# Four-layer graph transformer on one core: when layer 1's head inverses, logit rows and layer 0's expert selectors are computed

## The reference

```python
scores = jnp.sqrt(jax.nn.softplus(flat @ gate_w))
_, indices = jax.lax.top_k(scores + gate_bias, K)          # K = 2 of E = 8
combine = combine.at[jnp.arange(N)[:, None], indices].add(weights)
gate_h = jnp.minimum(jnp.einsum('td,edi->eti', flat, w1), LIMIT)
up_h = jnp.clip(jnp.einsum('td,edi->eti', flat, w3), -LIMIT, LIMIT)
h = jax.nn.silu(gate_h) * up_h
routed = jnp.einsum('etd,te->td', jnp.einsum('eti,eid->etd', h, w2), combine)
```

```python
h = (x @ W).reshape(n, heads, out_c)
al_s = jnp.einsum('nhc,hc->nh', h, a_src)
al_d = jnp.einsum('nhc,hc->nh', h, a_dst)
e = jax.nn.leaky_relu(al_s[src] + al_d[dst], 0.2)
m = jax.ops.segment_max(e, dst, num_segments=n)
ex = jnp.exp(e - m[dst])
z = jax.ops.segment_sum(ex, dst, num_segments=n)
out = jax.ops.segment_sum(h[src] * (ex / (z[dst] + 1e-16))[:, :, None], dst, num_segments=n)
```

## Time and profile before

| | us |
|---|---|
| median of three runs (lowest, highest) | 3343.7 (3342.97, 3345.96) |
| the profiled execution, its own time | 3345.06 |
| its span in the trace | 3343.3 |
| TensorE busy | 3091.6 (92%) |
| VectorE busy | 1723.2 (52%) |
| GpSimd busy | 1425.0 (43%) |
| ScalarE busy | 757.8 (23%) |
| mean granted TensorE clock | 0.95 |

### The profile page before, as it was taken

One profiled execution on the slowest core, in us unless ns is written; L12 is line 12 of the kernel. 1 busy time (PEld: TensorE's weight loads), 2 busy tenths in 40 slices (PEclk: granted clock), 3 DMA queues, 4 the chain that ended last, 5 costly groups with the idle time before them and its releaser, 6 DMA issues.

```text
span 3343.3 us, 39028 instructions
## 1 busy us (share of the span) xinstructions
PE 3091.6 (92%) x14135; PEld 2440.7 (73%) x14145; DVE 1723.2 (52%) x2812; ACT 757.8 (23%) x1342; POOL 1425.0 (43%) x1007
## 2 busy tenths in 40 slices
PE   8999899999999976998987889899999998989978
PEld 3576577788888864776776578578888886778858
DVE  7734699465655355447775446533334436641131
ACT  1044211333333122103153121211111102221222
POOL 2022288344433451653520034356666664536500
PEclk9999999999999988999987789999999999999987
DMA  2011266112211231221210231122332222213313
GB/s 81 15 48 43 90 215 205 62 58 76 67 57 57 71 99 35 81 85 62 66 34 10 65 112 60 59 85 90 99 99 94 94 89 66 70 47 101 94 43 120
DMA packets 92134, 259.38 MB, mean 78 GB/s; under 512 B 10431, under 2 KB 11071, under 8 KB 91716
## 3 DMA queue, kind: packets, MB, share of 16 engines
q1 hardware_dynamic: 80352, 219.45, 20.8%
q10 hardware_dynamic: 11652, 38.19, 3.4%
HBM read 256.03 MB, written 1.57 MB: 77 GB/s over the span
## 4 chain that ended last, share of the span: by engine, by line
PE 83%; DVE 10%; issue 3%; ACT 2%; DMA 0%; ACTq 0%; DVEq 0%
PE ps L427 22%; PE ps L431 21%; PE ps L432 21%; PE ps L909 2%; DVE aux L1963 2%; PE ps L535 1%; PE ps L529 1%; PE ps L1229 1%; PE ps L1125 1%; PE ps L788 1%; PE ps L799 1%; PE ps L781 1%; PE ps L773 1%; DVE hot L2398 1%; DVE row L1773 1%
## 5 line engine op out<-in xcount | busy, mean ns | idle before, releaser
L365 POOL TENSOR_SCALAR w_hi<-raw 128x768 fp32r<-128x768 f32 x498 | 457.8, 919 | 1701.2 <-PE ps L427 1459.8
L368 POOL TENSOR_TENSOR w_lo<-raw,w_hi 128x768 fp32r<-128x768 f32 x498 | 975.3, 1958 | 41.5
L427 PE MATMUL ps<-H_hi,w_hi 128*128 128x512 f32 x804 | 319.0, 397 | 21.1 <-issue 11.6
L427 PE MATMUL ps<-A_hi,w_hi 128*128 128x512 f32 x780 | 308.7, 396 | 17.6 <-DVE sel_now L2235 17.6
L431 PE MATMUL ps<-H_lo,w_hi 128*128 128x512 f32 x804 | 315.8, 393 | 0.0
L432 PE MATMUL ps<-H_hi,w_lo 128*128 128x512 f32 x804 | 315.7, 393 | 0.0
L427 PE MATMUL ps<-B_hi,w_hi 128*128 128x512 f32 x720 | 291.8, 405 | 21.0 <-DVE B_lo L1757 14.9
L431 PE MATMUL ps<-A_lo,w_hi 128*128 128x512 f32 x780 | 305.5, 392 | 0.0
L432 PE MATMUL ps<-A_hi,w_lo 128*128 128x512 f32 x780 | 304.6, 391 | 0.0
L431 PE MATMUL ps<-B_lo,w_hi 128*128 128x512 f32 x720 | 283.3, 393 | 0.0
L432 PE MATMUL ps<-B_hi,w_lo 128*128 128x512 f32 x720 | 283.0, 393 | 0.0
(11 more groups left out here) (477 smaller groups left out, 5882.6 us busy)
## 6 DMA issues: line engine op xcount, KB each, us to landing
raw<-stream_dram SPq DMA_DIRECT2D x558, 384.0 KB, 3.0
w_ring<-w_dram ACTq DMA_DIRECT2D x45, 384.0 KB, 3.7
u_rows<-rows_dram ACTq DMA_DIRECT2D x8, 768.0 KB, 5.6
rows<-rows_dram ACTq DMA_DIRECT2D x7, 768.0 KB, 3.9
w_last<-w_dram ACTq DMA_DIRECT2D x9, 384.0 KB, 3.5
x<-x_dram ACTq DMA_DIRECT2D x1, 1536.0 KB, 9.1
out_dram<-x ACTq DMA_DIRECT2D x1, 1536.0 KB, 5.1
orf<-orf_dram ACTq DMA_DIRECT2D x6, 192.0 KB, 3.0
```

The costliest lines, as they stand in the source:

```text
L365: pool.tensor_scalar(w_hi[:, b // 3, b % 3], raw[:, b // 3, b % 3], 1.0, 1.0, ALU.mult, ALU.mult)\
L368: pool.tensor_tensor(w_lo[:, b // 3, b % 3], raw[:, b // 3, b % 3], w_hi[:, b // 3, b % 3], ALU.subtract)\
L427: mm = pe.matmul(o, wh, xh, start=first, stop=False, skip_group_check=True)
```

## The change

- `experts0`: the copy of `sel_now` stands in front of `gat_vectors` of blocks 0 to 3 on VectorE, in the first round.
- In the projection, the source rows come two at a time: heads 0, 1 and the columns behind chunk 3, heads 2, 3 behind chunk 5, heads 4, 5 in the middle of tile 4, heads 6, 7 behind tile 5. The first `gat_targets` (bank 1 instead of 7) stands in the middle of tile 5 and the rows of head 0 behind it; the columns use bank 5.
- The features then hold only the second `gat_targets` and the rows of heads 1 and 2. The rows of head 3 stand behind them as before. ScalarE makes head 0's exponentials ahead of the first feature copy, heads 1 and 2 behind the second and third.
- The inverse of head `h` stands behind the weights of head `h + 2` (before: `h + 3`, and none before head 3's), the scaling of head `h` behind the exponentials of head `h + 4` (before: `h + 3`).
- `e_slope` has four buffers. Which head takes which is `slope_of`. ScalarE waits for the last head that had the same one.
- The merge is one `scalar_tensor_tensor` (smaller than 1, then larger) in place of a `tensor_tensor` (larger).
- The blocks owed to GpSimd are given back by a 2 x 2 matmul ahead of `gat_head_rows`, not by the transposes of `gat_targets`.

```diff
+        e_slope = [lambda m: edge_w[1][:, m], lambda m: exp_1[m // 2][:, 4 + m % 2], lambda m: exp_02[0][:, m],
+                   lambda m: exp_02[1][:, m]]
+        slope_of = [0, 1, 0, 1, 2, 3, 0, 1]
...
+            def gat_head_rows(h):
...
+                    if owed[0]:
+                        pe.matmul(ps[0:2, b, 0:2], ones_b[:, :], ones_b[:, :], start=True, stop=True,
+                                  skip_group_check=True).then_inc(w_used, owed[0])
+                        owed[0] = 0
...
+                def beside_projection(f, half=False):
+                    if (f, half) == (4, True):
+                        gat_source(4)
+                        gat_source(5)
+                    if (f, half) == (5, True):
+                        gat_targets(0, 1)
+                    if (f, half) == (5, False):
+                        gat_source(6)
+                        gat_source(7)
+                        gat_head_rows(0)
...
             def gat_exps(h):
-                if h >= 2:
-                    act.wait_ge(exps_merged, NT * (h - 1))
+                before = [u for u in range(h) if slope_of[u] == slope_of[h]]
+                if before:
+                    act.wait_ge(exps_merged, NT * (before[-1] + 1))
...
+                gat_exps(0)
                 for u in range(2 * NT):
                     gat_feature(u)
-                    if u in (1, 3, 5):
-                        gat_exps(u // 2)
+                    if u in (1, 2):
+                        gat_exps(u)
                 mark(act_to_pe)
-                for h in range(3, GAT):
+                gat_exps(3)
+                for h in range(4, GAT):
                     gat_exps(h)
-                    gat_scaled(h - 3)
+                    gat_scaled(h - 4)
...
-                        dve.tensor_tensor(e, e, e_slope[h % 2](m), ALU.max).then_inc(exps_merged, 1)
+                        dve.scalar_tensor_tensor(out=e, in0=e, scalar=1.0, in1=e_slope[slope_of[h]](m), op0=ALU.min, op1=ALU.max)\
+                           .then_inc(exps_merged, 1)
...
-                gat_vectors(range(4))
-                experts("experts0", 2, 10.0, True, lambda i: gat_vectors(range(4, KC)) if i == 0 else None)
+                experts("experts0", 2, 10.0, True, lambda n: gat_vectors((range(4), range(4, KC))[n]) if n < 2 else None)
...
-                gat_weights(0)
-                gat_weights(1)
                 gat_targets(1, 4)
-                for h in range(2, GAT):
+                for h in range(GAT):
                     gat_weights(h)
-                    if h >= 3:
-                        gat_inverse(h - 3)
+                    if h >= 2:
+                        gat_inverse(h - 2)
```

More of the change, by code:

```diff
@@ L936, in gat_terms @@
             def gat_terms():
-                pe.wait_ge(logits_out, 1)
-                use(7)
+                use(5)
                 for m in range(NT):
-                    mm = pe.transpose(ps[:, 7, m * 16:m * 16 + 16], row[0:16, m * P:m * P + P], ident[0:16, 0:16])
-                done(mm, 7, "dve")
+                    mm = pe.transpose(ps[:, 5, m * 16:m * 16 + 16], row[0:16, m * P:m * P + P], ident[0:16, 0:16])
+                done(mm, 5, "dve")
             def gat_source(h):
                 b = 6 + h % 2
+                if h == 0:
+                    pe.wait_ge(logits_out, 1)
                 use(b)
@@ L1073, in _, with behind_chunk @@
                 gat_logits()
-                turn_t(H, "dve", since, last=False,
-                       behind_chunk=lambda k: gat_terms() if k == 3 else gat_source(k - 4) if k >= 4 else None,
-                       halfway=lambda f: gat_source(f - 1))
+                def beside_projection(f, half=False):
[8 more added lines that the diff above has]
+                        gat_head_rows(0)
+                def behind_chunk(k):
+                    if k == 3:
+                        gat_source(0)
+                        gat_source(1)
+                        gat_terms()
+                    if k == 5:
+                        gat_source(2)
+                        gat_source(3)
+                turn_t(H, "dve", since, last=False, behind_chunk=behind_chunk, after=beside_projection,
+                       halfway=lambda f: beside_projection(f, True))
             if part("gnn1"):
                 def beside_features(t):
-                    if t == 0:
-                        gat_targets(0, 7)
-                        gat_source(5)
                     if t == 1:
-                        gat_head_rows(0)
-                        gat_source(6)
-                    if t == 2:
-                        gat_source(7)
-                    if t in (3, 5):
-                        gat_head_rows(t // 2)
+                        gat_targets(1, 4)
+                    if t in (1, 2):
+                        gat_head_rows(t)
                 gat_features(beside_features)
                 gat_head_rows(3)
-                gat_targets(1, 4)
                 pe.wait_ge(act_to_pe, S.due(act_to_pe))
@@ L1422, in gat_exps @@
                     e1 = act.activation(e_one[h % 4](m), ps[:, b], ACT.Exp, bias=al[:, 0, m, h:h + 1])
-                    e2 = act.activation(e_slope[h % 2](m), ps[:, b + 1], ACT.Exp, bias=gat_v[:, 3, m, h:h + 1])
+                    e2 = act.activation(e_slope[slope_of[h]](m), ps[:, b + 1], ACT.Exp, bias=gat_v[:, 3, m, h:h + 1])
                     if m < NT - 1:
@@ L2239, in expert @@
                         freed(dve.tensor_copy(row[:, :], ps[:, 6]), 6)
+                    if beside:
+                        beside(2 * i)
                     for j in range(KC):
@@ L2250, in expert @@
                     if beside:
-                        beside(i)
+                        beside(2 * i + 1)
                     add_t(x)
@@ L2510, in _ @@
                 gat_maxima(0)
+                gat_maxima(1)
+                gat_logit_columns()
                 add_t(x, "L1_mix_b_proj", range(3))
-                gat_maxima(1)
                 gat_maxima(2)
-                for f in range(3, KC):
-                    add_t(x, "L1_mix_b_proj", [f])
-                    if f < KC - 1:
-                        gat_maxima(f)
-                    if f == 3:
-                        gat_terms(0)
+                gat_maxima(3)
+                gat_terms(0)
+                add_t(x, "L1_mix_b_proj", [3])
+                gat_maxima(4)
+                gat_maxima(5)
+                add_t(x, "L1_mix_b_proj", [4])
+                gat_targets(0, 1)
+                add_t(x, "L1_mix_b_proj", [5])
             if "gnn1" in parts:
-                gat_targets(0, 7)
-                for h in range(5, GAT):
-                    gat_maxima(h)
+                gat_maxima(6)
+                gat_maxima(7)
                 gat_terms(1)
-                gat_weights(0)
-                gat_weights(1)
                 gat_targets(1, 4)
-                for h in range(2, GAT):
+                for h in range(GAT):
                     gat_weights(h)
-                    if h >= 3:
-                        gat_inverse(h - 3)
-                for h in range(GAT - 3, GAT):
+                    if h >= 2:
+                        gat_inverse(h - 2)
+                for h in range(GAT - 2, GAT):
                     gat_inverse(h)
```

12 lines of the change are left out of this document (4 added, 8 removed).

## The result

The changed kernel takes 3313.6 us (median of four executions, 3306.2 to 3323.3); the kernel before took 3343.8. The ratio is 0.9907, interval 0.9889 to 0.9924, that is 25 to 37 us gained. The forecast was 3322.0. The direction was right, the size was not: 30 us gained, not 21.7. One execution of the kernel before, of the 56 on record, took 4548 us at a mean clock of 0.64 and is left out everywhere.

What follows compares the result with a forecast made beforehand. TensorE, busy 92% of the span, bounds the kernel, so edits pay where it stands still or its clock rises. Gains 5.3 + 0 + 16.4 = 21.7 us from 3345.06 give 3323.4, as a median 3322.0; range 3313 to 3333.5.

Steps and rivals of the forecast that it cites:

- Selector: Layer 0's experts: the earlier copy lets TensorE start when ScalarE's SiLU frees bank 0, 5.3 us gained (4 to 6).
- Projection: Projection and features: same matmuls moved, stall spared against clock falls, 0 us (2.3 gained to 5 lost).
- VectorE's maxima: Projection: source-row pairs need both heads' maxima, at most 2.8 us a head; no stall expected, a wait would show it wrong.
- the 0.84 us: Projection: TensorE's only stall before product 0, ahead of a source row, goes.
- Heads: Layer 1's heads, product 0 to the transposes: 63.25 us falls to 46.9, 16.4 gained (11.5 to 20.2).
- the doubt about the Trainium skill's page: Heads' products: closed gaps would make them fast by that rule; trace agrees only in part, so middle 4.6 us taken.
- One figure beside the sum: Heads' merge: at the skill's half throughput the sum would be some 2 us worse; the trace's 0.69 us was used.
- the last one of the sum: Whole program: 21.7 us off the profiled 3345.06 gives 3323.4; runs' median 1.4 lower, so 3322.0.
- 1: Heads and projection: the clock eats part, all products slow and three more falls, 12.3 gained, 3331.4 us; chance 0.17.
- 2: Experts: bank 0 free without ScalarE's load wait, whole selector wait goes, 26.9 gained in all, 3316.8 us; chance 0.05.
- 3: Heads: no speedup, late scaling keeps 8.28 us per head; only the selector's gain left, 3338.4 us; chance 0.05.
- 4: Heads: waits close into one loop, 18.5 us per head for heads 4 to 7, 41 lost, 3379 us; chance 0.03.

Runs made afterwards that it cites:

- e2: Kernel before with only the selector copy moved ahead of the folding: 3345.2 us against 3349.8 on that chip, ratio 0.9988.
- e7: Kernel of e5 with only the new order ahead of the heads' loop and the new merge form: 3324.9 us, ratio 0.9922 to the kernel before.
- e10: Kernel of e5 with only the inverse of head h moved behind the weights of h + 2: 3312.4 us, ratio 0.9881 to the kernel before.
- e14: Kernel of e6 with the scaling of head h back behind the exponentials of h + 3 and two slope buffers: 3313.0 us, ratio 0.9895 to before.
- e15: Kernel of e6 unchanged, run again on one chip with others: 3311.7 us, ratio 0.9889 to the kernel before.
- e8: Kernel of e6 with the merge written as tensor_tensor again: 3309.6 us, ratio 0.9877 to the kernel before.
- e12: Kernel before with four unread matmuls behind the last stage of ffn3 instead of in the gap ahead of it: ratio 0.9997.
- e3: Changed kernel with the selector copy put back behind the folding: ratio 0.9927 to the kernel before, executions 3314.6 to 3331.6 us.
- e4: Kernel before with only the heads' loop changed (earlier inverses, later scalings, four slope buffers): ratio 0.9957, 14.4 us gained.
- e5: Kernel before with four unread matmuls in the 1.01-us gap ahead of the last stage of ffn3: 3329.1 us, ratio 0.9936.
- e6: Changed kernel with four unread matmuls in the gap ahead of the last stage of ffn3: 3309.5 us, ratio 0.9878 to the kernel before.
- e1: Changed kernel run again, unchanged: 3313.9 us, ratio 0.9904 to the kernel before, six executions from 3308.8 to 3327.3.
- e9: Kernel of e5 with the heads' loop changed (earlier inverses, later scalings, four slope buffers): 3315.0 us, ratio 0.9889 to the kernel before.
- e11: Kernel of e5 with only the scaling of head h moved behind the exponentials of h + 4: 3328.7 us, ratio 0.994 to the kernel before.

## Why the prediction was right or wrong

**Selector, 5.3 us forecast: right.** 5.5 us in the trace, by the mechanism named: the SiLU ends the wait, 12.1 us of it. The end-to-end gain is 1 to 7 us (e2), 3.5 to 4 by the stretches above.

**Projection, 0 forecast: right.** No wait for VectorE's maxima appeared, the 0.84 us went, and from the up tiles to product 0 the two traces take the same to 0.04 us. That nothing came of it is a balance, as the prediction said: with TensorE busy throughout, the clock is at 0.81 and 0.51 from 1665 to 1675, which costs 3.4 us against 1.7 before, and this is made up for, in part by the 0.84 us. The 7 us that the new order gives alone (e7) are mostly gained in the heads, and beside the earlier inverses nothing is left of them.

**Heads, 16.4 us forecast: the mechanism right, the size 2.9 too large in that trace, 13.5.** The working took 3.7 us for product 0 "as before" and 4.6 for the others. Product 0 and four more took 5.44 or above: closing the gaps did not lift the clock, which was granted at 0.50 to 0.84 from 1705 to 1740. Here the doubt about the Trainium skill's page "TensorE: Matmul & The Clock Gate" (section "What's actually happening"), by which activity releases the throttle, was in place: TensorE was fully busy in all these windows, and in 1720 to 1725 the clock stayed at its lower level throughout. The transposes behind gave 1.7 us back (2.81 for 4.48), which the sum had not counted. The forecast moved both the inverse and the scaling and did not say which carried the gain. The inverse alone carries it (e10), and in e14 against e15 the later scalings and the four buffers add nothing to it. One figure beside the sum was too small: by its own rows a merge at half rate would have taken VectorE from 5.9 to some 8.7 us per head against TensorE's 6.5, so some 2 us for each head from the point where its lead is used up, and not 2 in all. It did not come to that (e8).

**The step that failed is the last one of the sum:** that the rest of the program takes in the changed kernel what it took in the profiled execution of before, so that the median lies 1.4 us under it. A term was missing. The last stage of ffn3 took 41.19 us at a clock of 0.50 in the trace of before, behind a gap of 1.01 us, and so it did in e2 and e12, where it begins at 3270 and 3275. The change brings it to 3249 and 3252, and there one traced execution of the changed kernel has the stage slow and one fast, 17 us apart. Of its ten executions three are at 3323 to 3327 and seven at 3306 to 3317; eight of them have no trace and are placed by their times and mean clocks (0.951 or 0.952 in the three, 0.954 to 0.957 in the seven; the traced slow one has 0.952, the traced fast one 0.956). The time of the gap does not decide by itself: e3 and e4 have the stage at 3258.4 and 3258.6, the one fast, the other slow. Of the kernel before, too, one execution of 55 took 3333.1 at a mean clock of 0.953 where its neighbours on that chip took 3343.9 to 3355.1 at 0.946 to 0.950; it has no trace. With the stage fast in both kernels (e5, e6) 19.6 us remain of the 21.7 forecast. The 30.3 measured are 10.7 more; if the stage is fast in seven of ten executions, their mean gains seven tenths of 17.1, that is 12 us (an estimate). That filling the gap sets the stage's clock is shown (e5, e6, e12). Why, with the gap open, the clock falls in one execution and not in another is not; no run tells.

The rivals: 1 had the clock eat 9 us, and named the right place in the heads' products, but the stage that I had not looked at gave more than the clock took there. In 2 bank 0 comes free early, and it did not (ScalarE idles 31.02 us for `u_all`). Rivals 3 and 4 are out, since the heads take 49.7 us and not 63.25 or more.

## What to carry to other kernels

Before a sum is made from one trace, list the long dense stages with a clock of 0.50 and a short gap ahead of them: each can be a term with two values, which here took the one or the other in executions of one kernel. Filling the gap in both kernels with harmless matmuls takes that term out of the comparison; here it also was worth as much as the whole change.

Where engines wait for each other in a closed loop, try each moved line alone: here one edit did it all, and two others that gave 7 us each alone added nothing to it.

When two kernels differ by a few us, compare the same stretch in their traces as well as their times. Here the times lost a gain of 3.5 us in delays ahead of all edits.

## What the runs showed of the hardware that was not expected

- One stage, two levels: 192 matmuls of 64 columns without a stall take 21.62 us at a clock of 1.00 or up to 41.19 mostly at 0.50. Behind an open gap of 1.0 to 1.4 us it was slow in five traces (before, after, e2, e4, e12) and fast in two (e1, e3). With the gap filled it took 21.6 to 22.2 us in all ten.
- The gap is not the only source of spread: with it filled, six kernels stay within 7 us over their executions, but e9, e10 and e11 spread over 10.6 to 12 and e14 over 19. Part of it lies ahead of every edit: the 17 traces reach the transposes of `comb_n` between 1316.7 (before) and 1328.4 us (e14), and e12, which is the kernel before up to there, reaches them at 1324.1. What causes that was not found.
- A GpSimd instruction can last as long as a row of VectorE's: a copy that else takes 0.84 us took 5.14 when it met VectorE in a row of two-input passes at full rate (one each 0.60 us). It ended 0.7 us behind the last of these:

```profile
1693.77 1.28 DVE L2352 SCALAR_TENSOR_TENSOR exp<-exp,counts 128x512 f32<-128x512 f32 x2
```

In before the same meeting went the other way: GpSimd's copies took 0.84 to 1.28 us there, and VectorE's passes grew, one to 2.30 us beside a split of 2.36. What decides between the two was not found. I put it down to the form of the merge; e8 shows that it isn't. It cost nothing here: TensorE has no wait from 1635 to 1705.
